# Linear attention and a rounded projection on one core: intra moved right behind the inter product, their matmuls mixed, V behind both

## What is computed

```python
# attention: 64 heads of 8 values
q = softmax(exp(beta) * heads(xn @ Wq.T + bq), axis=-1)
k = softmax(exp(beta) * heads(xn @ Wk.T + bk), axis=-1)
v = heads(xn @ Wv.T + bv)
kv = cumsum(einsum('zsD,zsd->zsDd', k, v), axis=1)   # running state over the tokens
kn = cumsum(k, axis=1)
num = einsum('zsD,zsDd->zsd', q, kv)
den = sum(q * kn, axis=-1)
attention = (num / den) @ Wo.T + bo
# projection: xn is rounded to fp8 values first
projection = round_to_fp8(clip(xn / input_scale)) * input_scale @ (weight_fp8 * weight_scale).T + bias
```

## Time and profile before

| | before |
|---|---|
| median of 3 runs | 1248.71 us (1248.42 to 1251.34) |
| span of the profiled execution | 1248.2 us |
| PE busy | 1174.9 us, 94% |
| DVE busy | 977.9 us, 78% |
| ACT busy | 744.9 us, 60% |
| POOL busy | 321.6 us, 26% |
| granted TensorE clock, mean | 0.982 |

### The profile page before, as it was taken

How to read it: one execution, slowest core, us unless ns; L and a number is a source line. 1 busy time by engine, 2 the same in 40 slices (tenths; PEclk the granted TensorE clock), 3 DMA queues, 4 the chain that set the end, 5 groups by cost and what they waited for, 6 DMA issues and landing times.

```text
span 1248.2 us, 60447 instructions
## 1 busy us (share of the span) xinstructions
PE 1174.9 (94%) x26082; PEld 679.2 (54%) x26082; DVE 977.9 (78%) x1968; ACT 744.9 (60%) x1177; POOL 321.6 (26%) x590
## 2 busy tenths in 40 slices
PE   1459999999999999999999999999999999999996
PEld 1235555555555555555555555555555555555553
DVE  4567887888788788878878887788788778878873
ACT  0456656665666666566666656666665666566652
POOL 3122222322222232222223232222323232222310
PEclk9689999999999999999999999999999999999999
DMA  9022334334334433433333343343343433333331
GB/s 234 21 59 70 81 90 89 78 80 91 82 82 87 89 80 79 90 86 80 85 89 82 77 90 89 78 84 91 81 79 91 84 83 81 91 82 81 72 73 46
DMA packets 156483, 104.64 MB, mean 84 GB/s; under 512 B 111968, under 2 KB 128480, under 8 KB 156256
## 3 DMA queue, kind: packets, MB, share of 16 engines
q1 hardware_dynamic: 155536, 99.76, 35.7%
q10 hardware_dynamic: 720, 1.31, 0.4%
HBM read 40.20 MB, written 16.78 MB: 46 GB/s over the span
## 4 chain that ended last, share of the span: by engine, by line
PE 92%; issue 3%; DVE 2%; DMA 1%; ACT 1%; POOL 1%; SPq 0%; POOLq 0%; DVEq 0%; ACTq 0%
PE s_ps L900 10%; PE a_ps L917 7%; PE a_ps L1018 6%; PE a_ps L999 6%; PE k_ps L873 5%; PE vo_ps L975 5%; PE vo_ps L873 5%; PE k_ps L877 5%; PE k_ps L875 5%; PE vo_ps L884 4%; PE vo_ps L888 4%; PE vo_ps L886 4%; PE vo_ps L877 4%; PE vo_ps L875 4%; PE q_ps L877 4%; PE q_ps L873 4%
## 5 line engine op out<-in xcount | busy, mean ns | idle before, releaser
L521 ACT ACTIVATE q_heads<-qT,cst 128x512 f32<-128x512 f32 x256 | 163.9, 711 | 88.2 <-DVE qT L769 88.2
L407 POOL TENSOR_TENSOR y_sum<-y,y_magic 128x512 f32<-128x512 f32 x64 | 81.4, 1272 | 433.0 <-DVE y_magic L629 433.0
L506 ACT ACTIVATE w_own<-kT,cst 128x512 f32<-128x512 f32 x128 | 85.5, 715 | 166.7 <-DVE kT L711 166.7
L530 ACT ACTIVATE st_seqs<-st_run,cst 128x576 f32<-128x576 f32 x252 | 181.5, 797 | 0.5 <-DVE st_run L665 0.5
L671 DVE TENSOR_TENSOR att<-s_ps,cst 128x512 f32<-128x512 f32 x256 | 163.8, 682 | 0.4 <-PE s_ps L900 0.4
L400 POOL TENSOR_TENSOR x_split<-xn,x_split 128x512 f16<-128x512 f32 x64 | 74.1, 1158 | 291.6 <-ACT x_split L462 284.3
L900 PE MATMUL s_ps<-q_heads,w_own 64*64 64x128 f32 x4096 | 141.3, 275 | 0.6 <-DVE att L671 0.6
L900 PEld LDWEIGHTS s_ps<-q_heads,w_own 64*64 64x64 f32 x4096 | 110.4, 132 | 54.3 <-issue 54.2
L462 ACT ACTIVATE x_split<-xn 128x512 f16<-128x512 f32 x64 | 40.3, 630 | 126.7 <-DVE xn L618 126.7
L873 PE MATMUL k_ps<-w_hi,xT 128*128 128x512 f16 x256 | 98.9, 386 | 17.0 <-DMA xT<-x_split 12.3
L727 DVE TENSOR_TENSOR vp<-vo_ps,vp 128x512 f32<-128x512 f32 x64 | 44.3, 692 | 86.3 <-PE vo_ps L877 86.3
(11 more groups left out here) (136 smaller groups left out, 2287.8 us busy)
## 6 DMA issues: line engine op xcount, KB each, us to landing
v_groups<-vp SPq DMA_DIRECT2D x512, 36.0 KB, 3.1
x_in<-L_attn_x SPq DMA_DIRECT2D x64, 256.0 KB
x_res<-L_attn_x SPq DMA_DIRECT2D x64, 256.0 KB
out<-o_sb SPq DMA_DIRECT2D x64, 256.0 KB
w_own<-L_attn_Wk SPq DMA_DIRECT2D x1, 1024.0 KB, 13.0
w_own<-L_attn_Wq SPq DMA_DIRECT2D x1, 1024.0 KB, 15.0
w_own<-L_attn_Wv SPq DMA_DIRECT2D x1, 1024.0 KB, 16.5
att<-L_ffn_weight_fp SPq DMA_DIRECT2D x1, 1024.0 KB, 18.1
```

The source lines that it names most:

```text
L506: last = sc.activation(k_pairs[:, i.parity, :, c, :], kT[:, :, :], ACT.Copy, scale=pair_mask[:, c:c + 1])
L521: last = sc.activation(q_heads[:, i.parity, :, j, :], qT[:, i.parity, :, :], ACT.Copy, scale=head_mask[:, j:j + 1])
L530: last = sc.activation(st_seqs[:, i.parity, :, :, b, :].rearrange("p g j w -> p (g j) w"), st_run[:, :, :, :].rearrange("p g j w -> p (g j ...
```

## The change

On PE, V goes behind intra, and inter and intra become one stage: eight inter matmuls (those that clear their part of `a_ps`), then the waits for att_ready and v_moved, then 64 intra matmuls with one of the other eight inter matmuls ahead of every eight. On DVE, statistics and variances go ahead of output, magic behind add_state, and normalise_attention, until now at the head of the following body, ahead of scale_values. On POOL, root goes ahead of rounding.

```diff
@@ POOL
                 if (i + 1).exists():
                     low_input(i + 1)
-                    rounding(i + 1)
                 if i.parity == 0 and (i + PAIR).exists():
                     root(i + PAIR)
+                if (i + 1).exists():
+                    rounding(i + 1)
@@ DVE
                 t = i - 1
-                if (i - 2).exists():
-                    normalise_attention(i - 2)
                 if (i + 1).exists():
                     normalise(i + 1)
...
-                if (i + 1).exists():
-                    magic(i + 1)
                 if t.exists():
                     mask_scores(t, 2)
                     mask_scores(t, 3)
...
+                if (i + 3).exists():
+                    statistics(i + 3)
+                if i.parity == 0 and (i + PAIR).exists():
+                    variances(i + PAIR)
                 if (i - 2).exists():
                     output(i - 2)
                 if t.exists() and i.exists():
                     add_state(t)
-                if (i + 3).exists():
-                    statistics(i + 3)
-                if i.parity == 0 and (i + PAIR).exists():
-                    variances(i + PAIR)
+                if (i + 1).exists():
+                    magic(i + 1)
+                if t.exists():
+                    normalise_attention(t)
                 if i.exists():
                     scale_values(i)
@@ PE
+            def inter(t, n, gp, u, start):
+
+                g = G // 2 * n + GP * u + gp
+                return mm(a_rows[TOK * u:TOK * (u + 1), n, gp, :], qT[:, t.parity, g, :],
+                          st_seqs[:, t.parity, g].rearrange("p j b w -> p (j b w)"),
+                          start=start, stop=False, skip_group_check=True)
+
+            def intra(t, h, n, j, u):
+
+                cols = slice(GW * j + SP * VW * n, GW * j + SP * VW * (n + 1))
+                return mm(a_rows[TOK * u:TOK * (u + 1), h, :, cols], att[:, n, J * h + u, j, :],
+                          v_groups[:, t.parity, :, n, J * h + u, j, :], start=False, stop=True,
+                          skip_group_check=True)
...
                     for n in range(2):
-                        for gp in range(GP):
-                            for u in range(J):
-                                g = G // 2 * n + GP * u + gp
-                                mm(a_rows[TOK * u:TOK * (u + 1), n, gp, :], qT[:, t.parity, g, :],
-                                   st_seqs[:, t.parity, g].rearrange("p j b w -> p (j b w)"),
-                                   start=(gp == 0), stop=False, skip_group_check=True)
-                if i.exists():
-                    if fold:
-                        pe.wait_ge(fold_ready, 1)
-                    if (i - 2).exists():
-                        pe.wait_ge(o_ready, (i - 1).n)
-                    project(vo_ps, i, MV, seeded=False).then_inc(v_done, 1)
-                if t.exists():
+                        for u in range(J):
+                            inter(t, n, 0, u, start=True)
                     pe.wait_ge(att_ready, (t + 1).n * 4)
...
                     for h in range(2):
                         for n in range(SEQS // SP):
                             for j in range(J):
-                                cols = slice(GW * j + SP * VW * n, GW * j + SP * VW * (n + 1))
+                                if j % 2 == 0:
+                                    inter(t, h, 1, n * SP + j // 2, start=False)
                                 for u in range(J):
-                                    last = mm(a_rows[TOK * u:TOK * (u + 1), h, :, cols],
-                                              att[:, n, J * h + u, j, :],
-                                              v_groups[:, t.parity, :, n, J * h + u, j, :], start=False, stop=True,
-                                              skip_group_check=True)
+                                    last = intra(t, h, n, j, u)
                     last.then_inc(a_done, 1)
+                if i.exists():
+                    if fold:
+                        pe.wait_ge(fold_ready, 1)
+                    if (i - 2).exists():
+                        pe.wait_ge(o_ready, (i - 1).n)
+                    project(vo_ps, i, MV, seeded=False).then_inc(v_done, 1)
```

## The result

| | before | after |
|---|---|---|
| median | 1249.37 us (1248.42 to 1251.34) | 1319.41 us (1316.42 to 1320.17) |
| span of the profiled execution | 1248.2 us | 1317.1 us |
| granted TensorE clock, mean | 0.982 | 0.983 |

The ratio is 1.0552, interval 1.0537 to 1.0567: 70 us slower. The forecast was 1254 us, its range ended at 1290.

A forecast was written before the change was run, and what follows sets the result against it. PE's own sequence was taken as the bound: its stretch from last output matmul to K goes from 5.54 to 5.64 us, +0.10x62 = +6 on 1248.7, written as 1254 us. Range 1218 to 1290.

The forecast's parts named there:

- Step (1): V moved behind intra joins K on PE, two full-width stages: 0.31 entry into intra becomes 0.215, -0.095 us a step.
- Step (2): Inter and intra become one PE stage, so one exit from narrow tiles goes: -0.10 us a step.
- Step (3): Reordered DVE finishes the masks earlier, so PE's entry to inter falls from mean 0.45 to 0.31: -0.14 us a step.
- Step (4): PE's mixed inter and intra stage takes 2.64 us against 2.18 for the two separate stages: +0.46 us a step.
- the queue of 64: PE holds 64 instructions, places freeing only in order; this limits the mixed stage to 0.53 us per two groups.
- The second rival: Each inter blocks the columns beside it, PE looking few passes ahead: stage 2.85 to 3.2, 1267 to 1289 us; chance 0.22.
- upper bound of 3.5: Longest mixed stage on PE, if each inter blocks all behind it: 0.52+8x0.375 = 3.5 us, 1308 us in total.
- the faltering of the earlier trace: In before's intra and state stages, passes or weight loads pause near the 64th instruction; read as a full instruction queue.
- the 6 of the forecast: Total predicted loss over the whole kernel: +0.10 us on PE's stretch, times 62 steps, +6 us.
- What the moved steps meet: Later V, transposes, normalising and rounding on SP, DVE and POOL cause no wait as a rule, 0.3 us at worst.
- The named cover: About 1 us between rounding's reader on DVE being wanted and K's end; without it k_max would start late.
- The first rival: Array columns stay full in the mixed stage: 2.07 to 2.15 us, -0.43 a step, 1222 us; chance 0.34.

The follow-up runs named there:

- unmixed: The changed kernel with all 16 inter matmuls ahead of the 64 intra, V still behind both; 1283.07 us, ratio 1.0267.
- masks_first: The kernel before, PE untouched: on DVE magic behind output and quantise behind mask_state(0), on POOL root ahead of rounding; 1242.61 us, ratio 0.9934.
- dve_only: The kernel before with the change's places of statistics, variances and magic on DVE and root on POOL; PE and normalise_attention as before; 1258.54 us, ratio 1.0065.
- own_first: The changed kernel, but in each eight intra the two for the inter's own column come first; 1339.50 us.
- by_four: The changed kernel with four inter, one for each column, ahead of every 32 intra; 1295.13 us, ratio 1.0363.
- unmixed_late_round: All 16 inter ahead of 64 intra in the changed kernel, plus quantise on DVE moved behind mask_state(0); 1266.93 us, ratio 1.0114.

## Why the prediction was wrong, point by point

**Step (1), V joins K: right.** Forecast 0.215, and 0.22 in all steps.

**Step (2), one exit goes: borne out by the sum.** The stage of unmixed is 2.22 up to V, against the two stages of the earlier trace rows with both exits, 1.12 + 1.28 = 2.40; the second entry went with step (1). The 0.18 of it, 0.095 of (1) and 0.17 of (3) make 0.44, and unmixed's undisturbed step is 0.44 shorter.

**Step (3), the masks: right in after.** Forecast and found 0.31 in all steps. The gain was sized from two steps, 0.14; over all 62 of before the entry is 0.48, not 0.45, so it is 0.17. That this part wins time is shown by masks_first, 7 us. That it isn't free by itself is shown by dve_only: I had named PE's output stage as what is late next, and left out V's wait for output(i-2), which statistics and variances were now ahead of. In after the longer mixed stage hides it.

**Step (4), the mixed stage: wrong, 2.64 forecast, 3.30 less the exit of 0.10, or 3.20, found.** This is the step that failed first. I read from the earlier trace rows that the queue of 64 is the bound and that places come free in order; the columns' own depth I mentioned only in a rival, and thought that it "can't show more". The pace of two groups is 0.34 x 2 = 0.68 and not 0.53, because a group's second intra for the inter's own column finds that column full, and everything behind it is held until the inter is through. The second rival is in the main the mechanism that happened, though it let PE look ahead by a number of matmuls in all, where the runs fit a depth of each column: its 2.85 to 3.2 us for a short look-ahead holds the 3.20. Its own account with this stage ends at 1289; its upper bound of 3.5 was not reached, and own_first passed it only with an order made for that. I gave it 0.22 and the queue of 64 the most, since the queue explained the faltering of the earlier trace rows. That faltering is still unexplained, and a reason that explains an oddity is no measure of what bounds a different order. The miss of 0.56 is worth 35 us; with the 6 of the forecast that is 41, against 39 in the account.

**What had no step at all: the 27 us of gaps.** The range ended at 1290, and with the mixed stage of 3.30 alone after would have been near 1290. The gaps took it out of the range. The prediction moved 2.6 us of slow rows out from between two dense stages and asked what that does to buffers, DVE, POOL and SP, but not what it does to the feeding of PE itself. In the profile before only one row spoke of it, the instruction queue's, and no PE row carried a wait for it. I don't see how to have given it a size from before alone; a mention as a rival would have widened the range to the right side.

**What the moved steps meet: right for after.** In every undisturbed step the first intra comes 0.52 behind the first inter, which is the head's own length, so v_groups is never late. The wait of DVE on POOL's rounding, which the prediction covers with 1 us, is 1.8 us in 2 places in after, both in the run's first 84 us. In unmixed, where the stage is a microsecond shorter, that cover is gone, and it costs 10.8 us. The named cover was the right one.

**The first rival** (columns stay full, 2.07 to 2.15) is what unmixed and by_four show, 2.22 with the exit of 0.10, in an order without its uneven turns; its 1222 us none of them reached. unmixed_late_round's undisturbed steps alone would make 1248 - 27 = 1221. So the forecast gain of merging is there on PE, and the whole of it is given back at the 256th rows.

## What to carry to other kernels

Put narrow matmuls on the columns of the array in even turns: at equal instructions, the place of two of eight made 2.9, 3.3 or 3.9 us of a stage, so a "mix" should be one for each column and not one. Before joining dense stages, look at the page's row of the instruction queue, divide PE's rows by its packets, and ask how short a time so many rows get (here under some 3.3 us was the danger, if not the whole rule); a stage of slow, wide matmuls between narrow ones can be what keeps the instructions coming. When work is moved up on an engine, list who waits for what it passes: here V waited for output(i-2).

## What the runs showed of the hardware that I had not expected

- A 32-wide column takes little ahead: the lengths of five orders (2.22, 2.22, 2.91, 3.30, 3.91) fit one f32 matmul that runs and one that waits in each column, with everything behind a full column held up. It was tried only with f32 matmuls of 36 and 144 elements in four columns.
- The Trainium skill (TensorEngine Tiling (Array Packing), Key Properties) says that a change of the tiling mode drains the engine. A change from full width to narrow costs 0.31 between starts where two full-width matmuls are 0.215 apart, in every kernel here (0.10 more), which fits; changes between the two narrow shapes cost nothing that by_four could show (2.24 against 2.22).
- PE can stand for 0.45 to 2.5 us between starts at a 256th of its rows with no wait in the profile; the row behind starts 2.15 to 2.92 us after the instruction queue's packet.
- Such a gap can cost more than itself: behind three of 1.97 to 2.22 us idle the granted clock fell to 0.5 and the next V took 1.6 or 1.7 us longer. unmixed_late_round had gaps up to 2.5 us between starts and kept the full clock.
- Open: what starts such a packet; what causes the faltering at the 64th row; and whether the merged stage could be kept while the gaps are avoided, without 2.6 us of filling. No kernel tried that.
